# First attention layer of a four-layer block: transposes moved ahead of the scores, query projection in three passes

## What is computed

```python
x = x + jnp.tanh(g_xattn[0]) * _L0_xattn_ref(_layernorm(x, axis=-1), ctx_1024, Wq, Wk, Wv, Wo)

q = (query @ Wq.T).reshape(B, Tq, 16, 64).transpose(0, 2, 1, 3)      # Wq: 1024 x 128
k = (context @ Wk.T)...                                              # Wk: 256 x 128, heads repeated 4 times
v = (context @ Wv.T)...
scores = jnp.einsum('bhqd,bhkd->bhqk', q, k) / scale
out = jnp.einsum('bhqk,bhkd->bhqd', softmax(scores), v)
return out.reshape(B, Tq, 1024) @ Wo.T
```

## Time and profile before

| | us |
|---|---|
| median of 3 runs | 4140.32 |
| lowest, highest | 4138.98, 4145.28 |
| the profiled execution | 4144.88 |
| its span in the trace | 4143.1 |

### The profile page before, as it was taken

How to read it: one execution, slowest core, us unless ns; L and a number is a source line. 1 busy time by engine, 2 the same in 40 slices (tenths; PEclk the granted TensorE clock), 3 DMA queues, 4 the chain that set the end, 5 groups by cost and what they waited for, 6 DMA issues and landing times.

```text
span 4143.1 us, 98481 instructions
## 1 busy us (share of the span) xinstructions
PE 3394.9 (82%) x34530; PEld 2544.8 (61%) x34530; DVE 2661.7 (64%) x7872; ACT 1804.7 (44%) x5028; POOL 1068.0 (26%) x841
## 2 busy tenths in 40 slices
PE   6999978888887688887669976777449899999955
PEld 5777754555555455555669974545448677777744
DVE  4666647777776577776535548999722565656579
ACT  4666645665665333443213332222124455656521
POOL 1222222333332000002551004443630323232211
PEclk9999986777777666776779997777569999999966
DMA  2000010000000100001116761110045000000000
GB/s 92 8 8 8 8 25 7 6 6 6 6 6 6 72 17 15 15 15 21 35 45 220 255 239 32 31 32 24 20 145 193 14 13 10 13 11 12 9 16 25
DMA packets 159241, 180.11 MB, mean 43 GB/s; under 512 B 39136, under 2 KB 136160, under 8 KB 158432
## 3 DMA queue, kind: packets, MB, share of 16 engines
q1 hardware_dynamic: 146352, 142.62, 10.7%
q0 software_dynamic: 12288, 25.19, 2.0%
q10 hardware_dynamic: 432, 10.19, 0.6%
HBM read 65.58 MB, written 33.03 MB: 24 GB/s over the span
## 4 chain that ended last, share of the span: by engine, by line
PE 50%; DVE 22%; issue 9%; SPq 8%; POOL 4%; DMA 3%; ACT 2%; another core or an unknown queue 1%; DVEq 0%; POOLq 0%; ACTq 0%
PE ps L903 45%; SPq L631 7%; PE ps L1064 4%; DVE acc L1901 2%; DMA arena_a<-kT 1%; POOL route L875 1%; POOL scr L851 1%; DVE mx L1776 1%; DVE probs L1778 1%; DVE o_sb L1883 1%; DVE arena_b L1843 1%; DVE st L1647 1%; DVE x_sb L1631 1%; DVE vsmall L1851 1%
## 5 line engine op out<-in xcount | busy, mean ns | idle before, releaser
L903 PE MATMUL ps<-xcT,small 128*128 128x256 f32 x2176 | 626.3, 427 | 40.1 <-ACT xcT L1382 23.9
L881 POOL TENSOR_TENSOR probs<-probs,den 128x1024 f32<-128x1024 f32 x192 | 363.9, 1902 | 940.6 <-DVE den L1796 673.8
L903 PEld LDWEIGHTS ps<-xcT,small 128*128 128x128 f32 x2176 | 418.7, 207 | 256.2 <-issue 92.9
L903 PE MATMUL ps<-small,xcT 128*64 128x64 f32 (+6 forms) x2976 | 474.3, 391 | 62.5 <-DVE acc L1901 32.6
L865 POOL TENSOR_TENSOR rstd<-veps,neghalf 128x2 f32<-128x2 f32 (+1 forms) x192 | 146.4, 763 | 1356.6 <-DVE veps L1680 1152.8
L1448 ACT ACTIVATE pT<-ps 128x512 f32<-128x512 f32 (+1 forms) x576 | 302.3, 571 | 439.7 <-PE ps L1064 438.3
L903 PE MATMUL ps<-small,oT 128*64 128x128 f32 (+1 forms) x2304 | 331.5, 295 | 22.6 <-ACT oT L1463 16.7
L903 PE MATMUL ps<-arena_b,qT 64*64 64x64 f32 (+3 forms) x9288 | 323.4, 237 | 21.5 <-issue 14.2
L1064 PE MATMUL ps<-small,probs 128*128 128x128 f32 x2176 | 325.6, 295 | 17.8 <-ACT pT L1448 8.5
L903 PEld LDWEIGHTS ps<-small,oT 128*64 128x64 f32 (+1 forms) x2304 | 283.6, 155 | 83.7 <-issue 47.0
L1064 PEld LDWEIGHTS ps<-small,probs 128*128 128x128 f32 x2176 | 261.8, 151 | 111.4 <-issue 79.6
(11 more groups left out here) (268 smaller groups left out, 6409.9 us busy)
## 6 DMA issues: line engine op xcount, KB each, us to landing
wbuf<-parts SPq DMA_DIRECT2D x70, 704.0 KB, 3.5
wbuf<-parts_b SPq DMA_DIRECT2D x39, 512.0 KB, 3.0
arena_a<-kT SPq DMA_DIRECT2D x1024, 8.0 KB
scr_y<-acc SPq DMA_DIRECT2D x109, 128.0 KB, 3.4
xcT<-in_ctxT SPq DMA_DIRECT2D x96, 128.0 KB, 2.1
xcT<-scr SPq DMA_DIRECT2D x70, 128.0 KB, 2.2
xn<-scr SPq DMA_DIRECT2D x39, 128.0 KB, 2.2
arena_a<-in_w ACTq DMA_DIRECT2D x1, 4096.0 KB, 12.4
```

The source lines that it names most:

```text
L881: pool.tensor_tensor(pr, pr, rv[:, t, 0:nh].unsqueeze(2).to_broadcast([P, nh, S]), ALU.mult).then_inc(s_probs.sem, 1)
L903: return nc.tensor.matmul(o, lhsT, rhs, start=start, stop=stop, skip_group_check=True)
```

## The change

In the string of l0x, `F+` moves from behind `P0` to directly behind `T0-`, on all engines. The query weights (128x1024) are split once at the start of the layer: ACT writes the high part into `q_parts`, DVE the low part; PE and DVE wait for them. `F` of l0x no longer writes `xcT`: ACT writes the transposed rows' high part into `xhi`, then DVE, which had no share in F, waits for it, writes the low part into `xlo` and releases the bank. Each of the eight query products of a group becomes three `F32R` matmuls into the same bank. `q_parts` lies over columns of `arena_b` that l0x doesn't use; no other tile moves. Branches for layer L3X are in the code but never taken, as `split_layers` holds L0X alone.

```diff
     l0x = Layer(0, "l0x", stages(
-        "L++ T0- S0 T1- S1 P0 F+ A0- M++ Q0+ N0 K0+ A1- N1 Q1+ P1 Q2+ W0- Q3+ W1- V0+"),
+        "L++ T0- F+ S0 T1- S1 P0 A0- M++ Q0+ N0 K0+ A1- N1 Q1+ P1 Q2+ W0- Q3+ W1- V0+"),
...
+        with ExitStack() as shared:
+            sb_shared("under_q", [P, 2048])
+            q_parts = sb_shared("q_parts", [P, 2048])
...
+        s_xhi = step("s_xhi", l0x=1)
+        s_whi = ctx.enter_context(nc.semaphore("s_whi"))
+        s_wlo = ctx.enter_context(nc.semaphore("s_wlo"))
...
+        split_layers = (L0X,)
+        def halves(buf):
+            return as_r(buf[:, 0:1024]), as_r(buf[:, 1024:2048])
...
                 if layer is L0X:
                     pe.wait_ge(s_small, 16)
+                    pe.wait_ge(s_wlo, 1)
...
+            def mm3(o, weights, a, n, par):
+                hi, lo = (part[:, a:a + n] for part in halves(weights))
+                mm(o, hi, as_r(xhi[:, par, :]), stop=False)
+                mm(o, hi, as_r(xlo[:, par, :]), start=False, stop=False)
+                return mm(o, lo, as_r(xhi[:, par, :]), start=False)
...
                 if kind == "Q" and layer is not L2X:
                     for i in range(2):
                         c = 2 * j + i
-                        last = mm(o[:, i * GT:(i + 1) * GT], w(layer.name + "_wq")[:, c * P:(c + 1) * P], xT)
+                        if layer in split_layers:
+                            last = mm3(o[:, i * GT:(i + 1) * GT], q_parts, c * P, P, g.par)
+                        else:
+                            last = mm(o[:, i * GT:(i + 1) * GT], w(layer.name + "_wq")[:, c * P:(c + 1) * P], xT)
...
                 if layer is L0X:
                     act.wait_ge(s_small, 16)
                     act.wait_ge(s_const, 3)
+                    nc.scalar.activation(halves(q_parts)[0], w("l0x_wq"), ACT.Copy).then_inc(s_whi, 1)
                     nc.scalar.activation(tgate[:, :], w("gates"), ACT.Tanh).then_inc(s_tanh, 1)
...
+                    elif layer in split_layers:
+                        src = bank(b, GT)
...
+                        nc.scalar.activation(as_r(xhi[:, g.par, :]), src, ACT.Copy).then_inc(s_xhi.sem, 1)
...
                     dve.wait_ge(s_tanh, 1)
+                    dve.wait_ge(s_whi, 1)
+                    dve.tensor_tensor(halves(q_parts)[1], w("l0x_wq"), q_parts[:, 0:1024],
+                                      ALU.subtract).then_inc(s_wlo, 1)
...
+                elif kind == "F" and layer in split_layers:
+                    dve.wait_ge(s_xhi.sem, s_xhi.after(g, 0))
+                    if layer is L0X:
+                        b = wait_filled(fr, g, u)
+                        dve.tensor_tensor(as_r(xlo[:, g.par, :]), bank(b, GT), xhi[:, g.par, :],
+                                          ALU.subtract).then_inc(drained[b], 1)
```

More of the change, by code:

```diff
@@ L436, in build @@
         steps = [s_stats, s_aggr, s_veps, s_rstd, s_xn, s_rope, s_mx, s_masked, s_sub,
-                 s_exp, s_sum, s_rv, s_probs, s_route, s_rexp, s_acc, s_mix, s_relu, s_upd, s_rank, s_res]
+                 s_exp, s_sum, s_rv, s_probs, s_route, s_rexp, s_acc, s_mix, s_relu, s_upd, s_rank, s_res, s_xhi]
         ident = w("ident")
@@ L1380, in do @@
                                              scale=rms_gain[:, 0:1]).then_inc(drained[b], 1)
+                    elif layer in split_layers:
+                        src = bank(b, GT)
+                        if layer is L3X:
+                            src = xcT[:, g.par, 0:GT]
+                            nc.scalar.activation(src, bank(b, GT), ACT.Copy).then_inc(drained[b], 1)
+                            wait_drained(fr, g, u)
+                        nc.scalar.activation(as_r(xhi[:, g.par, :]), src, ACT.Copy).then_inc(s_xhi.sem, 1)
                     else:
@@ L1814, in do @@
                     mix(g)
+                elif kind == "F" and layer in split_layers:
[4 more added lines that the diff above has]
+                                          ALU.subtract).then_inc(drained[b], 1)
+                    else:
+                        dve.tensor_tensor(as_r(xlo[:, g.par, :]), xcT[:, g.par, 0:GT], xhi[:, g.par, :],
+                                          ALU.subtract).then_inc(s_xlo.sem, 1)
                 elif kind == "N":
```

## The result

The changed kernel takes 4128.4 us (median of 10 runs, 4125.8 to 4131.3), the kernel before 4140.7 beside it (10 runs, 4131.9 to 4148.5), 12.3 less. The ratio is 0.997, 95% interval 0.996 to 0.9979: about 0.3% faster. The profiled execution took 4130.1 us with a span of 4128.2.

The account below looks back on a forecast made before the run. In l0x the softmax chain bounds up to A1, PE from there. Per iteration +0.10 - 0.47 = -0.37 us; 30 give -11, start -1: -12 from 4140.3, so 4128, range 4110 to 4143.

Parts of the forecast that it names:

- What bounds the iteration: In l0x, the softmax chain sets the time from S0 to A1, PE from A1 to the next T0; iteration 17.23 us.
- The passes behind A1: Three-pass query products on PE after A1: Q1 with Q2 0.34 less, Q3 0.13 less, 0.47 us an iteration.
- Q0's 0.13: PE time saved on Q0 ahead of the wait for oT before A1: 0.13 us, counted as worth nothing.
- the third rival: Passes in l0x run slower than in l2f, one each 0.19 us: 23 us slower, 4163; chance 0.03.
- the Trainium skill's rule: On PE, weight loads overlap running matmuls only where row groups differ; full-array passes would cost about 0.21 us each.
- The move: F between T0 and S0: 0.27 off ACT's chain, 0.37 more on PE, net +0.10 us an iteration at A1.
- The low part: DVE's new xlo instruction before S0's maximum, 2.10 to 2.53 after T0: costs nothing while covered, otherwise 0.43 us an iteration.
- The cover of 0.24: Slack on DVE before S0's maximum, which can't start before 2.77 after T0: 0.24 us left to absorb xlo.
- Rival 2: xlo lands on DVE's chain and delays S0's maximum by up to 0.43 us: nothing gained, 4139 to 4142; chance 0.11.
- Start: Start of l0x: weight split hidden, F goes ahead in the first iteration with scores; 1 us gained, bounds 0 and 2.9.
- Rival 4: Clock falls after the 1.1 us wait before A1, up to 1.7 us a fall: 40 us slower, 4180; chance 0.08.
- The sum: Whole kernel: 30 iterations give -11 us, the start -1, together -12 us, to 4128 against the median 4140.3.

Follow-up runs that it names:

- e1: Kernel before with only F moved ahead of the scores, query products left in full precision: 4071.4 us against 4073.0, ratio 0.9997.
- e5: Changed kernel with A0, M and Q0 put before P0, and K0 before N0: 4117.5 us against 4145.5 for the kernel before, ratio 0.9934.
- e3: Changed kernel with DVE's low part computed once more into an unused buffer: 4065.3 us against 4073.0 for the kernel before, ratio 0.9983.
- e7: Changed kernel run again with nothing altered, as the mark for its batch: 4134.7 us against 4145.5 for the kernel before, ratio 0.9972.
- e2: Changed kernel with F put back behind P0, the split products kept: 4106.9 us against 4073.0 for the kernel before, ratio 1.0081.
- e4: Changed kernel with one pass of high parts instead of three per query product: 4126.3 us against 4073.0 for the kernel before, ratio 1.013.
- e8: e4 with 192 do-nothing semaphore increments at the start of PE's l0x code: 4116.0 us against 4147.0 for the kernel before, ratio 0.9924.
- e10: Changed kernel with 72 do-nothing semaphore increments at the start of PE's l0x code: 4220.6 us against 4142.7 for the kernel before, ratio 1.0187.
- e9: Changed kernel with 96 do-nothing semaphore increments at the start of PE's l0x code: 4128.6 us against 4147.0 for the kernel before, ratio 0.9957.
- e6: Changed kernel with only A0 and P0 swapped, K0 left behind N0: 4153.8 us against 4145.5 for the kernel before, ratio 1.0022.

## Why the prediction was right

The forecast was 4128 and the time is 4128.4, inside the range of 4110 to 4143, and faster by 0.3%, the outcome it gave 0.62. By its steps:

*What bounds the iteration.* Two stretches, the softmax chain up to A1 and PE from A1 on: confirmed. e1 removed the 0.61 gap and gained nothing; e5 shortened the chain in front of A1 and gained 0.53 an iteration. The 1.1 us wait before A1 with oT as releaser was predicted and is 1.12.

*The passes behind A1.* 0.47 predicted (0.34 for Q1 with Q2, 0.13 for Q3), 8.68 - 8.20 = 0.48 measured. Their size in l2f carried over: the 12 records of Q1 and Q2 go from 228.29 to 229.69, so the first takes 0.23 and the others 0.117 each, against 0.20 and 0.117 in l2f. Q0's 0.13 was counted as nothing because PE waits behind it; A1 didn't come earlier, so it was nothing. This settles the third rival: a weight load of these passes is 0.188 long (median), longer than the 0.117 between two starts, so loads and matmuls overlap here too, against the Trainium skill's rule that the prediction cites.

*The move.* This is the term that was mis-sized most: +0.10 predicted, -0.01 measured. I gave F's two transposes 0.37 on PE, the distance from F to the next start in the earlier trace rows. At the new place S0 starts 1.24 after T0 instead of 1.02, so F costs 0.22 there: it starts 0.93 after T0, and S0 comes 0.31 after F, while T0 to S0 without F already held 1.02. The 0.27 off ACT's chain and the 0.22 on PE's nearly cancel, which is also what e1 shows (17.23 to 17.17). The bounds of 0.00 to +0.20 just missed it. With it the iteration is 0.49 shorter by these two terms, and 0.52 by the count of 30, instead of 0.37.

*The low part.* xlo predicted to end 2.53 after T0, measured 2.61; it starts 0.13 after xhi's end where I took 0.03. The maximum was due at 2.77 and came at 2.66, because S0 was earlier than I thought. The cover of 0.24 was about 0.14 by e3. Rival 2 didn't come, but it was nearer than the prediction has it.

*Start.* -1 predicted, -1.0 measured. In e7, the same kernel run again, the first T0 starts at 52.02, which is -0.7; e1, the move alone, has it at 50.33. Q2 waits for DVE's K0 copy there, as it said, and the granted clock is at its lower level for a while (0.59 on average from 47 to 50 us). Timeline of PE in the first iteration with scores:

```profile
44.40 0.39 PE L916 MATMUL ps<-xhi,q_parts 128*128 128x256 f32 x1 [1.48 <-ACT qT L1418]
...
47.69 0.58 PE L916 MATMUL ps<-xhi,q_parts 128*128 128x256 f32 x1 [2.31 <-DVE arena_b L1866]
48.07 0.41 PE L916 MATMUL ps<-xlo,q_parts 128*128 128x256 f32 x1
48.28 0.63 PE L916 MATMUL ps<-xhi,q_parts 128*128 128x256 f32 x2
...
51.74 1.09 PE L1088 MATMUL ps<-small,probs 128*128 128x128 f32 x8
```

The second pass and the third lie 0.21 apart instead of 0.117.

*The clock.* Rival 4 had 0.08, and its mechanism is real: e2 shows it with a gap of 1.98 in 9 of 30 iterations, e4 in 6 iterations. In the changed kernel with 1.12 the clock held, as the window in the earlier trace rows with a gap of that length had suggested.

*The sum.* -12 predicted; -12.3 between the medians and -14.9 between the two profiled executions. This agreement is worth less than it looks. Up to the next layer 17.9 were gained, six more than forecast (l0x's last steps behind the last T0 gave 1.2 of them), and 3 us of it came back in layers that the change doesn't touch, by the clock at the end of l1x. Two misses of opposite sign lie under the total: the iterations' 15.7 instead of 11, of which the move is 3.3, and the clock, which the prediction didn't look for outside l0x. That the total came out so near was in part luck.

## What to carry to other kernels

Idle time that the profile names in front of one instruction is a gain only if nothing behind it waits for another chain: here 0.61 before Q0 turned into 1.05 before A1 and the time stayed the same. Ask for each step from which engine the next buffer comes free, and price work that is taken off PE only between the last wait on another engine and the loop's end. When a step is faster, look at the longest gap it leaves and at how much the code of the engine moved: both can cost more than the step gives. And where unchanged code takes another time, compare the granted clock over the same instructions before looking for any other cause: the mean over a long stretch can hide it.

## What the runs showed of the hardware beyond this

- The position of code: the same l3x loop costs 80 us (e4 against e8) to 93 us (e10 against e9) more in the traces where, by my count, its code touches one more block of 256 instructions; the profile shows it as 205 or 206 packets on the instruction queue instead of 89, and as PE idle with "issue" as releaser, up to 2.85 us in one piece. The prediction didn't weigh this at all, though the change lengthens PE's code ahead of l3x by 0.38 blocks (72.24 to 72.62). 72 instructions more ahead of that loop, 0.28 of a block, and it would have been 2% slower (e10).
- The clock: with a gap of 1.98 in each iteration it fell to 1.2 GHz in 9 of 30 iterations, 1.56 us each (e2); with one of 1.67 in six iterations (e4). With a gap of 1.12 it stayed at 2.4 GHz from 150 to 450 us. The same 55 matmul records took 9.66 us where it rose among them and 13.39 where it stayed at 1.2 GHz.
- From the end of ACT's xhi to the start of DVE's xlo it took 220.95 - 220.43 - 0.39 = 0.13 us here and 0.04 in l2f of the kernel before (3059.17, 0.38 long, and 3059.59). Back to back on DVE, two subtractions of 0.42 start 0.34 apart.
- What stays open: l1f takes another time in other runs of unchanged code. From the first to the last write of ring it is 160.0 in the kernel before and 159.9 in the changed one, 163.8 in e7, the changed kernel again, and 118.9 in e1. When it starts has nothing to do with it as far as these runs show: e5, e7 and e6, run beside each other, write masked the first time at 1310.1, 1327.7 and 1347.2 and take 1135.0, 1134.7 and 1135.5 to the second write. No run here tells the cause.
